# A selective scan over four directions on one core: one division of work for the first three directions, and y stored by columns in runs of eight

## What is computed

```python
xs = jnp.stack([x_hw, x_wh, x_hw[..., ::-1], x_wh[..., ::-1]], axis=1)
x_dbl = jnp.einsum('bkdl,kcd->bkcl', xs, x_proj_w)
dts, Bs_, Cs_ = jnp.split(x_dbl, [R, R + N], axis=2)
dts = jnp.einsum('bkrl,kdr->bkdl', dts, dt_w)
delta = jax.nn.softplus(dts + dt_b[None, :, :, None])
def step(h, xs_t):
    d_t, u_t, B_t, C_t = xs_t
    dA = jnp.exp(d_t[..., None] * A)
    h = h * dA + (d_t * u_t)[..., None] * B_t[:, :, None, :]
    y = jnp.einsum('bkdn,bkn->bkd', h, C_t)
    return (h, y)
```

## Time and profile before

| | us |
|---|---|
| median of 3 runs | 14696.03 |
| lowest and highest of them | 14689.11, 14702.75 |
| the profiled execution | 14691.09 |
| its span | 14689.3 |
| DVE busy in the span | 12970.4 (88%) |
| PE busy | 13181.2 (90%) |
| ACT busy | 11123.1 (76%) |
| POOL busy | 10326.6 (70%) |

### The profile page before, as it was taken

How to read it: one execution, slowest core, us unless ns; L and a number is a source line. 1 busy time by engine, 2 the same in 40 slices (tenths; PEclk the granted TensorE clock), 3 DMA queues, 4 the chain that set the end, 5 groups by cost and what they waited for, 6 DMA issues and landing times.

```text
span 14689.3 us, 247142 instructions
## 1 busy us (share of the span) xinstructions
PE 13181.2 (90%) x65256; PEld 8153.8 (56%) x65256; DVE 12970.4 (88%) x13833; ACT 11123.1 (76%) x22914; POOL 10326.6 (70%) x4126
## 2 busy tenths in 40 slices
PE   6888988889888998889988899888998889988899
PEld 4566455664556645566455664556645566455654
DVE  8999689996899978999689996899969999599995
ACT  5888578885788857887578876788767887678875
POOL 6999069980699807998079970899708996099960
PEclk9999999999999999999999999999999999999999
DMA  3443023430343303443033430344303442043420
GB/s 114 129 131 124 25 93 128 130 124 21 97 130 129 119 21 102 130 141 103 21 111 128 140 96 21 116 130 138 91 21 123 131 138 83 21 131 128 138 78 26
DMA packets 907982, 1468.60 MB, mean 100 GB/s; under 512 B 38912, under 2 KB 891904, under 8 KB 893664
## 3 DMA queue, kind: packets, MB, share of 16 engines
q1 hardware_dynamic: 906560, 1452.37, 31.2%
HBM read 1350.07 MB, written 102.17 MB: 99 GB/s over the span
## 4 chain that ended last, share of the span: by engine, by line
PE 33%; issue 24%; POOL 16%; DVE 15%; ACT 7%; DMA 2%; DVEq 1%; ACTq 1%; POOLq 0%; SPq 0%
POOL area L1794 12%; DVE area L1229 9%; PE ps L756 7%; PE ps L1030 5%; PE ps L1042 5%; DVE area L1257 4%; PE ps L743 3%; POOL area L1804 3%; PE ps L734 3%; ACT ps L1554 3%; DMA area<-bc_rows 2%; PE ps L892 2%; ACT area L1523 2%; PE ps L724 2%; PE ps L856 1%
## 5 line engine op out<-in xcount | busy, mean ns | idle before, releaser
L1229 DVE TENSOR_TENSOR_SCAN area<-ps,hst,area 128x384 f32<-128x384 f32 x9216 | 8581.8, 994 | 150.5 <-ACT ps L1554 69.6
L1794 POOL TENSOR_TENSOR area<-area 128x1152 f32<-128x1152 f32 x3072 | 7998.3, 2638 | 62.6 <-POOL area L1779 29.4
L1554 ACT ACTIVATE ps<-area,a_neg 128x384 f32<-128x384 f32 x9216 | 5259.7, 580 | 984.8 <-DVE area L1229 959.2
L756 PE MATMUL ps<-area,ident 128*128 128x384 f32 x11472 | 4127.3, 494 | 441.5 <-POOL area L1804 408.2
L756 PEld LDWEIGHTS ps<-area,ident 128*128 128x128 f32 x11472 | 2050.0, 191 | 1918.6 <-POOL area L1804 449.4
L743 PE MATMUL ps<-ident,area 128*128 128x128 f32 x20736 | 2882.2, 275 | 0.0
L743 PEld LDWEIGHTS ps<-ident,area 128*128 128x128 f32 x20736 | 2604.0, 192 | 50.3 <-ACT area L1523 1.5
L1523 ACT ACTIVATE area<-ps,area 128x384 f32<-128x384 f32 x3456 | 1972.6, 571 | 560.2 <-PE ps L734 559.4
L1714 ACT ACTIVATE area<-ps,t_neg,area 128x768 f32<-128x768 f32 x1728 | 1617.8, 986 | 1001.1 <-PE ps L1030 1001.1
L1774 POOL TENSOR_TENSOR area<-area,ones 128x2304 f32<-128x2304 f32 x16 | 85.2, 5352 | 3103.5 <-ACT area L1483 2980.9
L734 PE MATMUL ps<-ident,area 128*128 128x128 f32 x10368 | 1765.2, 279 | 326.4 <-ACT area L1523 314.0
(11 more groups left out here) (163 smaller groups left out, 9539.6 us busy)
## 6 DMA issues: line engine op xcount, KB each, us to landing
area<-bc_rows SPq DMA_DIRECT2D x1536, 768.0 KB, 6.7
xz<-x_normed SPq DMA_DIRECT2D x144, 288.0 KB, 6.3
area<-in_x SPq DMA_DIRECT2D x18, 1728.0 KB, 10.1
area<-x_padded SPq DMA_DIRECT2D x24, 1250.0 KB, 12.1
z_raw<-z_st SPq DMA_DIRECT2D x144, 192.0 KB, 6.2
area<-z_raw SPq DMA_DIRECT2D x8, 3456.0 KB, 14.9
x_padded<-x_st SPq DMA_DIRECT2D x120, 200.0 KB, 7.8
x_normed<-area SPq DMA_DIRECT2D x9, 1728.0 KB, 8.1
```

Source lines behind the costliest of these rows:

```text
L756: m = e.matmul(ps[:, 5 + j, 0:CH], ident[:], hb[:, i % NH, j], start=i == 0, stop=i == N - 1)
L1229: e.tensor_tensor_scan(rev(hb[:, i % NH, j], k), rev(ps[:, 2 + j, 0:CH], k), rev(dbu[:, i % NH, j], k), hst[:, i, j:j + 1], ALU.mult, ALU. ...
L1554: e.activation(ps[:, 2 + j, 0:CH], dlt[:, par, j], ACT.Exp, scale=a_neg[:, j, k, i:i + 1]).then_inc(da, 1)
L1794: e.tensor_tensor(dbu[:, i % NH], du[:, par], row_b[:, q % 2, i % ROWS:i % ROWS + 1].broadcast_to([128, J, CH]), ALU.mult).then_inc(dbus, 1)
```

## The change

A third plan, LATE, replaces FIVE in directions 0 and 1 and SEVEN in direction 2: POOL 0, 6, 11; turned 1, 3, 4, 7, 10, 12, 13; DVE 2, 5, 8, 9, 14, 15; units at slots 12 and 13. Direction 3 keeps SEVEN.

`slot` changes for slots with two tiles. Sums of POOL states stood ahead of the first tile; they now stand behind it, with those of DVE states. Then comes a new place, `between`, ahead of the second tile: the add of y goes there (it stood behind the whole slot), and a unit of slot 13. Slots with one tile keep their order.

The first unit of LATE waits until all three deltas of the next step are made; the second waits until ACT has copied out the first. In ACT the ln of part 2 waits for the product of state 9 and no longer for a unit, and the copy of C for state 14 waits for the last delta. Some semaphore counts are kept in registers now, with the same values.

`y_chunk` and `y_psum` of directions 1 and 3 now both run over h outside and the eight w inside: SBUF addresses come in runs of eight, PSUM addresses 48 elements apart. Before, they ran over w outside and h inside: SBUF 48 elements apart, PSUM straight.

```diff
+        self.late = units[0] > 11
+        self.ln_free = max(n for n in self.dve if n < 10)
+        self.after_ln = {5: 1, 8: 2, min(n for n in self.dve if n > 10): 3}
...
-FIVE = Plan((0, 3, 6, 9), (1, 4, 7, 10, 13), (10, 14))
 SEVEN = Plan((0, 6, 9), (1, 3, 4, 7, 10, 12, 13), (10, 13))
-PLANS = (FIVE, FIVE, SEVEN, SEVEN)
+LATE = Plan((0, 6, 11), (1, 3, 4, 7, 10, 12, 13), (12, 13))
+PLANS = (LATE, LATE, LATE, SEVEN)
...
+assert S_ALL % NC == 0 and all(not p.slots[N + 1] and max(map(len, p.slots.values())) < 3 for p in PLANS)
...
-    return b * S_ALL + (LAST.ns + S_TO[q] + n)
+    return b * NC * (S_ALL // NC) + (LAST.ns + S_TO[q] + n)
...
-            return y_v.rearrange("p j (h w) -> p j w h", h=H)[:, :, ds(c * 8 if k < 2 else (NC - 1) * 8 - c * 8, 8), :]
+            return y_v.rearrange("p j (h w) -> p j h w", h=H)[:, :, :, ds(c * 8 if k < 2 else (NC - 1) * 8 - c * 8, 8)]
...
-            return p if k % 2 == 0 else p.rearrange("p j (w h) -> p j w h", w=8)
+            return p if k % 2 == 0 else p.rearrange("p j (w h) -> p j h w", w=8)
...
-                def slot(q, m):
+                def slot(q, m, between=None):
 
                     p = plan(q)
-                    for i in p.order:
-                        if p.sum_at[i] == m and i in p.pool:
-                            state_sum(q, i)
+                    sums = [i for i in p.order if p.sum_at[i] == m]
+                    if len(p.slots[m]) < 2:
+                        for i in sums:
+                            if i in p.pool:
+                                state_sum(q, i)
                     for at in p.slots[m][:1]:
                         tile(q, at)
                     if m == N + 1:
                         turned_sum(q, p.nt - 1)
-                    for i in p.order:
-                        if p.sum_at[i] == m and i in p.dve:
+                    for i in sums:
+                        if i in p.dve or len(p.slots[m]) == 2:
                             state_sum(q, i)
+                    if between:
+                        between()
                     for at in p.slots[m][1:]:
                         tile(q, at)
 
+                def add_y(k, c, m):
+                    if m in ADD_AT:
...
                     e.wait_ge(hcs, made_d(b, q, plan(q).dve.index(plan(q).unit_after[i]) + 1))
+                    if i == 1:
+                        e.wait_ge(unit_ev, h * 2 + 1)
+                    elif plan(q).late:
+                        e.wait_ge(dp_v, b * 72 + (3 * q + 6))
                     e.wait_ge(xz_in, h * 16 + 16)
                     for t in range(CT):
                         at = i * DI + k * 128
                         m = e.matmul(ps[:, 1, 0:CH], w_in[:, t, at:at + 128], xz[:, t], start=t == 0, stop=t == CT - 1)
                     m.then_inc(unit_mm, 1)
 
+                def filler(k, c, h, q, m):
+                    add_y(k, c, m)
+                    if k < UK and m == 13 and m in plan(q).units:
+                        unit(k, h, q, plan(q).units.index(m))
+
...
-                        if k < UK and m in plan(q).units:
+                        if k < UK and m in plan(q).units and m != 13:
...
-                        slot(q, m)
+                        slot(q, m, lambda: filler(k, c, h, q, m))
                         if m < 3 and m in LATE_X and not last:
                             x_proj(1, LATE_X[m])
-                        if m in ADD_AT:
-                            j = ADD_AT[m]
-                            if k == 0:
-                                e.matmul(ps[:, 5 + j, 0:CH], d_diag[:, j], u_v[:, 0, j, ds(pos(k, c), CH)],
-                                         start=False, stop=False)
-                            else:
-                                e.matmul(y_psum(k)[:, j], ident[:], y_chunk(k, c)[:, j], start=False, stop=False)
...
-                    if nxt and i in (5, 8, 11):
-                        e.wait_ge(dp_v, g * 3 + (3 + (i - 2) // 3))
+                    if nxt and i in plan(q0).after_ln:
+                        e.wait_ge(dp_v, g * 3 + (3 + plan(q0).after_ln[i]))
...
-                            softplus(g + 1, 1 - par, nxt[0], "ln", LN_AT[i], h=h if i == 11 else None,
-                                     c8=made_d(b, q, plan(q).dve.index(8) + 1))
+                            softplus(g + 1, 1 - par, nxt[0], "ln", LN_AT[i], h=h if i == 11 and not plan(q).late else None,
+                                     c8=made[q] + (plan(q).dve.index(plan(q).ln_free) + 1))
```

More of the change, by code:

```diff
@@ L774, in slot @@
                         turned_sum(q, p.nt - 1)
-                    for i in p.order:
-                        if p.sum_at[i] == m and i in p.dve:
+                    for i in sums:
+                        if i in p.dve or len(p.slots[m]) == 2:
                             state_sum(q, i)
+                    if between:
+                        between()
                     for at in p.slots[m][1:]:
                         tile(q, at)
+                def add_y(k, c, m):
+                    if m in ADD_AT:
+                        j = ADD_AT[m]
+                        if k == 0:
+                            e.matmul(ps[:, 5 + j, 0:CH], d_diag[:, j], u_v[:, 0, j, ds(pos(k, c), CH)],
+                                     start=False, stop=False)
+                        else:
+                            e.matmul(y_psum(k)[:, j], ident[:], y_chunk(k, c)[:, j], start=False, stop=False)
                 def unit(k, h, q, i):
                     e.wait_ge(hcs, made_d(b, q, plan(q).dve.index(plan(q).unit_after[i]) + 1))
+                    if i == 1:
+                        e.wait_ge(unit_ev, h * 2 + 1)
+                    elif plan(q).late:
+                        e.wait_ge(dp_v, b * 72 + (3 * q + 6))
                     e.wait_ge(xz_in, h * 16 + 16)
@@ L788, in unit @@
                     m.then_inc(unit_mm, 1)
+                def filler(k, c, h, q, m):
+                    add_y(k, c, m)
+                    if k < UK and m == 13 and m in plan(q).units:
+                        unit(k, h, q, plan(q).units.index(m))
                 def body(k, c, par, last, nxt):
-                    g = e.snap(b * 24 + (c + k * NC))
                     q = k * NC + c
@@ L1494, in scan_phase @@
             def scan_phase(b):
+                tiles, made = {}, {}
                 def hold_state(k, c, i):
@@ L1512, in c_copy @@
                     e.wait_ge(c_in[q % 2], g * 32 + (16 * (q // 2) + 16))
-                    e.wait_ge(hcs, made_d(b, q0, d))
+                    e.wait_ge(hcs, made[q0] + d)
                     e.activation(ps[:, 1, 0:CH], row_c[:, q % 2, i % ROWS], ACT.Copy).then_inc(c_ps, 1)
@@ L1520, in turned_product @@
                     t = c * 3 if k < 2 else (NC - 1) * 3 - c * 3
-                    e.wait_ge(turn_mm, made_t(b, q, at + 1))
-                    e.wait_ge(turn_sum, made_t(b, q, at - 2))
+                    e.wait_ge(turn_mm, tiles[q] + (at + 1))
+                    e.wait_ge(turn_sum, tiles[q] + (at - 2))
                     e.activation(ht[:, at % 3], ps[:, 0, 0:CH], ACT.Copy,
@@ L1540, in store_y @@
                         e.wait_ge(ysum, made_s(b, k * NC + c, plan(k * NC + c).ns))
-                    e.wait_ge(turn_sum, made_t(b, k * NC + c, plan(k * NC + c).nt))
+                    e.wait_ge(turn_sum, tiles[k * NC + c] + plan(k * NC + c).nt)
                     e.activation(y_chunk(k, c)[:, j], y_psum(k)[:, j], ACT.Copy).then_inc(yev, 1)
@@ L1547, in body @@
                     h = e.snap(b * UC + (c + k * NC)) if k < UK else None
+                    tiles[q], made[q] = e.snap(made_t(b, q, 0)), e.snap(made_d(b, q, 0))
                     e.wait_ge(dp_v, g * 3 + 3)
```

## The result

The changed kernel took 14801.32 us (median of 4 runs, 14793.41 to 14804.12) against 14694.49 us before on the same chips: ratio 1.007, 95% interval [1.0055, 1.0085]. It is slower by 107 us; the forecast was 86 (14780, range 14660 to 14850). The profiled execution's span is 14799.8 us, 110.5 more than before.

What follows compares the result with a forecast made beforehand. DVE was taken as the spine, POOL beside it in directions 0 and 1. Per-image terms +4.9, +2.5, +5.8, -1.7 and -0.7 net +10.8 us, +86 over 8 images: 14782, stated as 14780 us, range 14660 to 14850.

Steps and rivals of the forecast that it cites:

- The bound and the sum of a step: Directions 0 to 2: DVE is the spine; a LATE step takes 52.95 + 2.1 = 55.05 us.
- the stall of 2.1 us: Before scan 15 of each LATE step: DVE waits 2.1 us for PE's sum of state 11.
- scan 15 at +7.57: LATE steps: scan 15 starts 7.57 us after scan 13's start, against +5.46 without the wait.
- Direction 2's wait of 1.01 us for ACT: Before scan 15 in direction 2: DVE's 1.01 us idle time behind ACT's second turned product goes.
- The units: Slot 13, second unit: runs +1.5 to +2.9 us after scan 13's start, just before the turn; cost taken as 0.
- The faster rival: At scan 15: the sum of state 11 isn't last, no stall, 14480 us (14638 at a 1.1 stall); chance 0.2.
- the break-even at a stall of 1.5 us: Whole kernel: the change neither gains nor loses if LATE steps stall 1.5 us; each 0.1 us is worth 14.4 us.
- Runs of eight: Store of y, directions 1 and 3: falls to the straight price, 488 ns, removing 0.34 us at state 3.
- the third rival: Stores and adds of y: strided PSUM costs the same or more, +38 us, 14820; chance 0.25.
- My price of 0 for moving the add in slot 5: Slot 5: `add_y` ahead of the second tile costs 0, as an add is 0.7 us and PE waits anyway.
- the first step: Direction 0, first step of an image, 60.2 us before: -1.25 + 2.1 = +0.9 us.
- The stores at an image's end: End of each image, direction 3: the three bare stores of y save 0.7 us.

Runs made afterwards that it cites:

- Sum first: The changed kernel with POOL's sum of state 11 put back ahead of the first tile of slot 14: 14612.98 us, ratio 0.9943 to the kernel before.
- a third of the sum: The changed kernel with PE summing only the first of three parts of state 11 in directions 0 to 2: 14609.74 us, ratio 0.9939.
- ACT's copies ahead: The changed kernel with state 11's sum in slot 13, second unit in slot 14, ACT's copies before its last turned product in iteration 15: 14552.27 us.
- y alone: The kernel before with only the new y addresses of `y_chunk` and `y_psum`: 14685.57 us against 14697.77, ratio 0.9993.

## Why the prediction was right

**The bound and the sum of a step: right.** The step of 55.05 us came out at 55.00, the stall of 2.1 us at 2.12, scan 15 at +7.57 as walked. Sum first and a third of the sum show that this sum was the cause: the wait moves with the sum's place and with its length. POOL fell to 51.9 us and stopped no one in the steps of directions 0 to 2. Direction 2's wait of 1.01 us for ACT is gone. The chain had been put together from three places of the trace of before: the tiles' times in direction 3, the length of a sum in direction 2, and the 0.12 us from a sum's end to a scan in an image's first step. Each link of it is one instruction that waits for one other, and each took here what it took there.

**The units: right, narrowly.** The second unit was put from +1.5 to +2.9 ahead of a turn at +3.08; measured are 2481.45 (+1.39) to a turn at +3.07. The turn still waited for ACT (0.19 us), not for the unit.

**The faster rival: shown wrong as stated, right as a condition.** The sum does end too late by the order written. At a stall of about 0.9 us, as in sum first, the forecast's own rate (14.4 us per 0.1) gives 14801 - 176 = 14625, and 14613 was measured; the break-even at a stall of 1.5 us lies between the two measured stalls. With no wait for the sum at all the rival has 14480; the kernel nearest to that, with ACT's copies ahead, took 14552, as 0.45 us a step came up elsewhere.

**Runs of eight: right for the store, and the add came out at its lower bound.** I took the straight price for the store, left the adds between the straight price and today's, and let the third rival have them at 813 ns or more. A PSUM operand stepped by 192 bytes, with SBUF in runs of 8, costs a matmul nothing here: 486 ns. This is against what the Trainium skill says (Advanced Engine Details and Errata, PSUM Cachelines: any non-contiguous pattern in PSUM significantly slows down matmuls); for these fp32 matmuls of 384 columns the measurement decides. It was SBUF's step of 192 bytes that cost. My price of 0 for moving the add in slot 5 hung on that without saying so: it went by an add of 0.7 us, and with the old add of 1.45 us the move costs 0.30 us in 12 steps of an image, 29 us in all. The third rival kept the adds at 813 ns and left this out, so its 14820 was too low: with the old addresses 14855 was measured.

**The terms that were mis-sized: an image's first step, and what lies outside the scan phases.** The forecast was 86 us, of which 92 in the scan phases and -6 at the images' ends; the spans differ by 110.5. The scan phases account for 97.3 (10486.6 against 10389.3), what lies outside them for 13.2.

In the scan phases the term that is far off is the first step: +0.9 us forecast, +2.3 measured as mean of eight (60.0 to 62.3 us), 11 us in all. The others together came out 0.7 us per image below their forecast, 6 us in all, so the near miss of the phases (97 against 92) is in part luck. The windows of two first steps, the first sum on PE of each, and the waits on DVE in the first of them:

```profile
1988.89:2051.60 62.71, 54.81 (x279) 36.81 (x279) 56.68 (x74) 46.85 (x107) 54.74 (x22) 0.97 0.47 148
12979.00:13040.02 61.02, 54.00 (x282) 36.53 (x281) 56.59 (x75) 46.84 (x107) 54.76 (x22) 1.00 0.50 155
...
2004.86 3.62 PE L760 MATMUL ps<-area,ident 128*128 128x384 f32 x6 [1.58 <-DVE area L1210]
...
12994.97 2.20 PE L760 MATMUL ps<-area,ident 128*128 128x384 f32 x6 [1.58 <-DVE area L1210]
...
2008.61 5.65 DVE L1247 TENSOR_TENSOR_SCAN area<-ps,hst,area 128x384 f32<-128x384 f32 x6 [2.71 <-PE ps L760]
2015.13 0.55 DVE L1196 SCALAR_TENSOR_TENSOR area<-area,ps 128x384 f32<-128x384 f32 x1 [0.87 <-ACT ps L1489]
...
2022.93 2.83 DVE L1247 TENSOR_TENSOR_SCAN area<-ps,hst,area 128x384 f32<-128x384 f32 x3 [0.41 <-PE ps L738]
...
2047.61 2.83 DVE L1247 TENSOR_TENSOR_SCAN area<-ps,hst,area 128x384 f32<-128x384 f32 x3 [2.04 <-PE ps L760]
```

The waits for the first sum (2.71) and for state 11's (2.04) were in the forecast; 0.87 and 0.41 us are new, and they make up most of the difference. In between, the two more tiles of state 3 come right behind the late first sum, ACT's products are late by them, and its ln stands behind those. I have argued this from the trace; no run isolates it. With y alone, without the new plan, the first step stays at 60.0 us.

Two images out of eight had a first step of 61.0 us instead of 62.7, and in the kernel before one had 58.7 instead of 60.2. These are the steps with a granted clock of 1.00 throughout: the first state sum takes 2.20 us in them, and 3.15 to 3.89 in the others, where the lower level (0.5) falls on it and the window has 0.97. The two new waits are there at either clock (0.70 and 0.41 us in the window at 12979.00), and at like clocks the step grew by 2.3 and 2.5 us. So the clock isn't what was mis-sized.

Outside the scan phases the code is the same but for the addresses of the last stores. The seven stretches between the scan phases of two images (two of them and the sum; the third number from the end is the granted clock), in the changed kernel:

```profile
5132.91:5651.99 519.08, 505.99 (x2386) 239.40 (x2386) 326.55 (x324) 295.52 (x359) 20.16 (x25) 0.98 0.09 26
...
8795.20:9317.14 521.94, 508.83 (x2385) 240.33 (x2385) 326.82 (x324) 295.74 (x359) 20.14 (x25) 0.97 0.09 26
...
sum 3646.70, PE 3555.18 PEld 1679.24 DVE 2287.71 ACT 2070.11 POOL 140.96; mean PE 507.88 PEld 239.89 DVE 326.82 ACT 295.73 POOL 20.14
```

In the kernel before:

```profile
6914.31:7431.66 517.35, 503.79 (x2385) 238.32 (x2385) 326.80 (x324) 296.43 (x359) 20.12 (x25) 0.99 0.09 26
8730.64:9250.63 519.99, 506.44 (x2385) 239.16 (x2385) 326.62 (x325) 296.20 (x359) 20.13 (x25) 0.98 0.09 26
...
sum 3635.32, PE 3540.49 PEld 1673.40 DVE 2287.23 ACT 2073.78 POOL 140.91; mean PE 505.78 PEld 239.06 DVE 326.75 ACT 296.25 POOL 20.13
```

And in the sum-first kernel, which has the changed kernel's code there too:

```profile
10481.01:10997.26 516.25, 503.24 (x2384) 238.19 (x2383) 326.67 (x325) 295.64 (x359) 20.12 (x25) 0.99 0.09 26
...
sum 3625.24, PE 3533.56 PEld 1671.34 DVE 2287.09 ACT 2069.71 POOL 140.81; mean PE 504.79 PEld 238.76 DVE 326.73 ACT 295.67 POOL 20.12
```

DVE's and POOL's busy times are the same to 0.4 us, ACT's are about half a us lower with the new addresses; the stretch is 516 to 517 us where the granted clock averages 0.99 and about 522 where it is 0.97. The changed kernel's execution had 3646.7 us of them, the one before 3635.3, sum-first 3625.2. Sum-first was below the kernel before with the changed kernel's code, so this part is no cost of the change. It goes with the share of PE's lower clock level (1.2 of 2.4 GHz) that an execution happens to get there: by the granted clock in the traces, 116 us of these stretches were at the lower level in sum-first, 133 in the kernel before and 177 in the changed kernel. The six other traces lie between, from 3629.7 us with 120 at the lower level to 3645.4 with 171. The stores at an image's end, forecast at -0.7, are in here too: their three records took 2.08 us from 3280.62 before and 1.57 us from 3307.32 after, where the third now waits 0.15 for PE, so -0.5. What decides how often the clock falls, and whether the medians carry the same share as the profiled executions, I haven't tested.

## What to carry to other kernels

Where the reuse of a buffer depends on a sum, ask by which microsecond of the waiting engine's own pace the sum must end, and walk the program order of the engine that makes it up to that point. Here PE had 6 us of air per step and still cost DVE 2.1 us by one sum 2 us long, 1.2 of them because it stood behind a tile instead of ahead of it. A gain that relieves two loaded engines is only worth what the next ordered wait leaves, so place that wait before counting the gain. Ask too whether work that is moved into an engine's idle time still fits there: the same add cost DVE nothing at 0.81 us and 0.30 us at 1.45.

## What the runs showed of the hardware

- A matmul of 384 fp32 columns and ACT's copy of them from PSUM take the same time (486 and 487 ns) with the PSUM side straight or stepped by 192 bytes per element, when the SBUF side is in runs of 8 elements. With the step of 192 bytes on the SBUF side they take 813 and 828.
- A state sum (six matmul records) takes 2.20 us in an image's first step at a granted clock of 1.00, and 3.62 us in one where the clock falls to 0.5 during it.
- With practically the same code between scan phases, one such stretch takes 516.3 to 522.9 us with the granted clock. Over the seven of an execution the nine traces differ by up to 21 us (3625.2 to 3646.7), more than the 12 us measured for y alone.
